# Gated cross-attention and ternary FFN on one core: a schedule moved by one or two slots, and two jobs given to other engines

## What is computed

```
h   = ln(layernorm(x)) ; xq = fp8(clip(h / in_scale))        # four versions: q, qx, k, v
q,qx,k,v = xq @ {wq,wqx,wk,wv}.T ; kx,vx = ctx @ w_kv_x.T     # 16 heads, 8 kv groups, D=128
core = softmax(ln(q) ln(k)^T / sqrt D) v ; xout = softmax(ln(qx) ln(kx)^T / sqrt D) vx
x1  = x + tanh(g0) * (fp8(clip([core, xout] / smooth)) @ wproj.T) * scale
out = x1 + tanh(g1) * down(silu(a) * b), with a,b = quant(layernorm(x1)) @ ternary(w_gate_up).T
```

## Time and profile before

| | |
|---|---|
| median of 3 runs | 1841.8 us (1840.5 to 1842.0) |
| the profiled execution | 1840.5 us, span 1838.4 us |
| busy over the span | PE 1629.0 us (89%), DVE 1536.1 (84%), ACT 1371.2 (75%), POOL 1099.4 (60%) |
| mean granted TensorE clock | 0.971 |
| first `scores` (slot 0) | 111.24 us |
| feed-forward stage | from about 1490 us to the end |

### The profile page before, as it was taken

One profiled execution on the slowest core, in us unless ns is written; L12 is line 12 of the kernel. 1 busy time (PEld: TensorE's weight loads), 2 busy tenths in 40 slices (PEclk: granted clock), 3 DMA queues, 4 the chain that ended last, 5 costly groups with the idle time before them and its releaser, 6 DMA issues.

```text
span 1838.4 us, 35220 instructions
## 1 busy us (share of the span) xinstructions
PE 1629.0 (89%) x11147; PEld 1007.6 (55%) x11164; DVE 1536.1 (84%) x3391; ACT 1371.2 (75%) x3439; POOL 1099.4 (60%) x1421
## 2 busy tenths in 40 slices
PE   2368889889999999999999888999999978999995
PEld 1345555555666665666666555666666534444442
DVE  7568889999897899988788999999988847777774
ACT  6458999879989988998997788989988832222222
POOL 3577888878886787888676667767777520000000
PEclk9889999999999999999999999999999989999998
DMA  3257789779999999999898988999998976322200
GB/s 102 90 148 166 185 189 211 166 181 228 228 227 200 199 242 191 210 232 245 189 222 177 210 195 201 235 226 223 225 232 168 211 166 214 91 73 77 70 18 17
DMA packets 669596, 325.48 MB, mean 177 GB/s; under 512 B 552288, under 2 KB 595424, under 8 KB 669152
## 3 DMA queue, kind: packets, MB, share of 16 engines
q1 hardware_dynamic: 669408, 323.17, 77.5%
HBM read 140.61 MB, written 48.23 MB: 103 GB/s over the span
## 4 chain that ended last, share of the span: by engine, by line
PE 43%; DVE 23%; ACT 13%; POOL 8%; issue 8%; DMA 4%; SPq 0%; ACTq 0%; POOLq 0%; DVEq 0%
PE psum L699 8%; PE psum L654 7%; PE psum L687 7%; PE psum L741 6%; PE psum L716 6%; DVE pp L981 5%; DVE nmx L971 4%; PE psum L661 3%; PE psum L758 3%; DMA pt<-pp 2%; ACT pp L1321 2%; ACT psum L1310 2%; PE psum L674 2%; ACT raw L1241 2%; DVE xh L954 1%
## 5 line engine op out<-in xcount | busy, mean ns | idle before, releaser
L687 PE MATMUL psum<-qk 128*128 128x512 f16 x1536 | 423.6, 385 | 19.5 <-DVE pp L981 13.4
L699 PE MATMUL psum<-pt,vv 128*128 128x512 f16 x1536 | 402.1, 385 | 36.9 <-ACT cy L1329 25.3
L654 PE MATMUL psum<-wbt,xqt 128*128 128x256 f16 (+1 forms) x4096 | 409.2, 249 | 21.5 <-DVE xqt L898 11.1
L1310 ACT ACTIVATE psum<-psum,nmx 128x512 f32<-128x512 f32 x512 | 352.3, 688 | 70.2 <-DVE nmx L971 68.7
L654 PEld LDWEIGHTS psum<-wbt,xqt 128*128 128x128 f16 x4096 | 330.2, 99 | 135.5 <-issue 18.1
L981 DVE SCALAR_TENSOR_TENSOR pp<-psum,prs,pp 128x512 f16<-128x512 f32 x512 | 379.4, 741 | 3.4 <-ACT pp L1321 3.3
L971 DVE TENSOR_REDUCE nmx<-psum 128x1 f32<-128x512 f32 x512 | 345.6, 675 | 31.1 <-PE psum L687 30.6
L1321 ACT ACTIVATE pp<-psum,prs 128x512 f16<-128x512 f32 x512 | 365.7, 714 | 6.7 <-DMA pt<-pp 6.5
L699 PEld LDWEIGHTS psum<-pt,vv 128*128 128x128 f16 x1536 | 147.9, 99 | 236.5 <-issue 55.1
L1564 POOL TENSOR_TENSOR qk<-y,qk 128x512 f16<-128x512 f32 x192 | 232.5, 1211 | 16.0
L687 PEld LDWEIGHTS psum<-qk 128*128 128x128 f16 x1536 | 144.0, 99 | 103.9 <-DVE pp L981 23.1
(11 more groups left out here) (176 smaller groups left out, 2792.8 us busy)
## 6 DMA issues: line engine op xcount, KB each, us to landing
wbt<-ws SPq DMA_DIRECT2D x192, 256.0 KB, 3.7
ws<-wbt SPq DMA_DIRECT2D x64, 256.0 KB, 4.0
catd<-cy SPq DMA_DIRECT2D x64, 256.0 KB, 3.3
raw<-in_wgu SPq DMA_DIRECT2D x64, 256.0 KB, 3.5
raw<-in_w SPq DMA_DIRECT2D x32, 384.0 KB, 3.9
wbt<-catd SPq DMA_DIRECT2D x6, 2048.0 KB, 9.8
pt<-pp SPq DMA_TRANSPOSE x512, 3.8
raw<-in_wp SPq DMA_DIRECT2D x32, 256.0 KB, 3.7
```

Of the source, the lines that this page charges most:

```text
L654: ins = e.matmul(bank[:, o0:o0 + c1 - c0], xv[:, v, kt * 512 + tt * 128:kt * 512 + (tt + 1) * 128], wb[i][:, h, kt, c0:c1], start=kt == 0 ...
L687: ins = e.matmul(SB(n), qk[i][:, jq, u, ss], qk[i][:, jk, w, :], start=k == 0, stop=k == 2)
L699: ins = e.matmul(OB, v[:, t, u, att, :], src[:, w, t, :], start=t == 0 and k == 0, stop=t == 3 and k == 2)
L1310: e.activation(SB(n), SB(n), ACT.Exp, bias=nmx[:, k], accum_out=psm[:, k]).then_inc(s["exp"], 1)
```

## The change

Most edits are numbers in the tables. `FIRST` and the ramp's loads go two slots earlier with `GEMM_AT` (9 to 7), so that the projections of a group come two slots earlier against its scores; one of them, the load of weight tile 3 of group 1, now comes before the two kv loads instead of between them. The first head of a group goes one slot earlier, the x transposes one or two slots later, the second product with v of a head block moves from the second to the third of its four slots. `norm_b` is done by DVE up to B tile 35 (group 8) instead of 7 (group 1), so for 28 tiles the two ACT copies go. In a split job `hi` goes from ACT to POOL and `lo` from POOL to DVE, in the same slots as before.

```diff
-FIRST, PAST = -26, NSLOT + 20
+FIRST, PAST = -28, NSLOT + 20
-PVS = ((0,), (1, 2), (3,), ())
-GEMM_AT = 9
+PVS = ((0,), (1,), (2, 3), ())
+GEMM_AT = 7
-HEADS_AT = (10, 12, 14, 16, 18, 22)
-FACTORS_AT = 6
+HEADS_AT = (9, 12, 14, 16, 18, 22)
+FACTORS_AT = 4
-RAMP_LOAD = (-27, -26, -25, -20, -20, -19)
-W0_AT = -22
+RAMP_LOAD = (-29, -28, -27, -22, -20, -19)
+W0_AT = -24
-STORE_W = 10
+STORE_W = 8
-ACT_NORM = 2 * 4
-WG_AT, CAT_AT, X2_AT = (444, 490), (474, 498), 507
+ACT_NORM = 9 * 4
+WG_AT, CAT_AT, X2_AT = (444, 488), (472, 496), 506
-SCALE_AT = {"sum": 303, "whole": 308, "fac": 309}
+SCALE_AT = {"sum": 303, "whole": 307, "fac": 308}
-    "turn": (19, 24, 35, 51),
+    "turn": (20, 26, 36, 52),
-    "parts": (104, 104, 104, 104),
+    "parts": (102, 102, 102, 102),
@@ sp_program
-                nw, j = divmod(n + 7 + 2 * SLOTS, SLOTS)
+                nw, j = divmod(n + 8 + 2 * SLOTS, SLOTS)
@@ pe_program, gemm
-                            q.wait_ge("w_dn", it * 6 + (6 if it > 1 else 4))
+                            q.wait_ge("w_dn", it * 6 + (6 if it else 4))
@@ dve_program, job: the tern branch as before, and
+                else:
+                    q.wait_ge("l_hi", JV["l_hi", m])
+                    if stored is not None:
+                        q.wait_ge(f"l_st{i}", JV[f"l_st{i}", stored])
+                        q.wait_ge("l_ab", JV["l_ab", summed])
+                    e.tensor_tensor(o.bitcast(F16)[:, 0:512], f, wps[:, j, :], ALU.subtract).then_inc(s["l_lo"], 1)
@@ act_program: job_hi is gone, and its call in slot n
-                e.activation(wps[:, j, :], raw[i][:, 0:512], ACT.Copy).then_inc(s["l_hi"], 1)
@@ pool_program, job: the subtraction is gone; called in slot n instead of n + 1
+                    q.wait_ge(f"raw_ld{i}", JV[f"raw_ld{i}", K0 + m])
+                    e.tensor_scalar(wps[:, j, :], raw[i][:, 0:512], 1.0, 1.0, ALU.mult, ALU.mult).then_inc(s["l_hi"], 1)
```

More of the change, by code:

```diff
@@ L998, in job @@
             def job(m):
-                if JOBS[m][0] != "tern":
+                what, src, j, _ = JOBS[m]
+                i = (K0 + m) % 2
+                f, o = raw[i][:, 0:512], raw[i][:, 512:768]
+                if what in ("sum", "scale"):
                     return
-                i = (K0 + m) % 2
-                f, ob = raw[i][:, 0:512], raw[i][:, 512:768].bitcast(BF16)[:, 0:512]
                 stored, summed = JB[m]
[L1004 to L1008, removed]
+                if what == "tern":
+                    ob = o.bitcast(BF16)[:, 0:512]
+                    q.wait_ge("l_t1", JV["l_t1", m])
+                    q.wait_ge(f"l_st{i}", JV[f"l_st{i}", stored])
+                    q.wait_ge("l_ab", JV["l_ab", summed])
+                    q.done(e.tensor_scalar(ob, f, MAGIC, 1.0, ALU.subtract, ALU.min))
+                    e.tensor_scalar(ob, ob, -1.0, None, ALU.max).then_inc(s["l_t2"], 1)
+                else:
+                    q.wait_ge("l_hi", JV["l_hi", m])
+                    if stored is not None:
+                        q.wait_ge(f"l_st{i}", JV[f"l_st{i}", stored])
+                        q.wait_ge("l_ab", JV["l_ab", summed])
+                    e.tensor_tensor(o.bitcast(F16)[:, 0:512], f, wps[:, j, :], ALU.subtract).then_inc(s["l_lo"], 1)
             def weight_sums():
@@ L1330, in o_out @@
                              scale=f).then_inc(s["o_y"], 1)
-            def job_hi(m):
-                j, i = JOBS[m][2], (K0 + m) % 2
-                q.wait_ge(f"raw_ld{i}", JV[f"raw_ld{i}", K0 + m])
-                e.activation(wps[:, j, :], raw[i][:, 0:512], ACT.Copy).then_inc(s["l_hi"], 1)
             def job(m):
@@ L1416, in act_program @@
                     ctx_hi(b, kt)
-                if JOB_AT.get(n, -1) >= 0 and JOBS[JOB_AT[n]][0] == "split":
-                    job_hi(JOB_AT[n])
                 for at in (n, n - 2):
@@ L1580, in job @@
                 i = (K0 + m) % 2
-                f, o = raw[i][:, 0:512], raw[i][:, 512:768]
                 if what == "split":
[L1583 to L1588, removed]
+                    q.wait_ge(f"raw_ld{i}", JV[f"raw_ld{i}", K0 + m])
+                    e.tensor_scalar(wps[:, j, :], raw[i][:, 0:512], 1.0, 1.0, ALU.mult, ALU.mult).then_inc(s["l_hi"], 1)
             q.wait_ge("pre_v", 1)
@@ L1642, in pool_program @@
                         ctx_lo(b, kt)
-                if JOB_AT.get(n - 1, -1) >= 0:
-                    job(JOB_AT[n - 1])
+                if JOB_AT.get(n, -1) >= 0:
+                    job(JOB_AT[n])
             weights_over(q)
```

## The result

The changed kernel takes 1861.6 us (median, 1856.6 to 1868.2) against 1841.2 for the kernel before on the same chip: ratio 1.0116, 95% interval 1.0098 to 1.0136, so about 21 us slower. I had predicted 1835, with a range of 1823 to 1846.

What follows compares the result with a forecast made beforehand. ScalarE was taken as fullest in groups 1 to 3, 9 and 17, VectorE in 4, 5 and 12 to 14. Terms summed to -7.1 us, giving 1834.7 from the median, predicted as 1835; 8-in-10 range 1823 to 1846.

Steps and rivals of the forecast that it cites:

- ramp and end: Before slot 0 and in groups 30 and 31: gemm parts done earlier, 1.0 us gained at each.
- VectorE has 3 us or more of room in most, so nothing is counted: Groups 7, 8, 10, 11, 15, 16, 18: split subtractions cost nothing; 0.5 us gained in 10 and 11.
- Rival 2: Groups 6, 12 to 14 and 4 to 6: subtractions queue behind GpSimd on full VectorE, 1847 us; chance 0.18.
- the gains in groups 9 and 17: Two and three split copies leave a full ScalarE: gains of 1.5 and 1.7 us, low end 0.
- the 1.05 assumed: Length in us taken for each new VectorE subtraction of a split job, with ends 0.69 and 1.66.
- The rule of the Trainium skill quoted in the prediction: VectorE instructions with two SBUF inputs and GpSimd instructions reading SBUF exclude each other; the second is blocked throughout. No term.
- What the prediction read from ctx_lo: Slow cases of the similar subtraction overlap GpSimd instructions; its spread, 686 to 1662 ns, agrees with mutual blocking.
- the fullest engine plus a smaller loss: Groups 1 to 3: time is the fullest engine plus 2 or 1 us per group; gains 4.3 and 4.7 us.
- rival 1: Groups 1 to 3: wait moves to the broadcast, VectorE bounds at once; gain 3 instead of 9, 1841 us; chance 0.20.
- their work is the same and stands at the same distance from it: Tables `FACTORS_AT`, `STORE_W`, `load_w`, `parts`, `SCALE_AT` follow the gemm, so they were counted at nothing.
- PVS at nothing: Last `pv` of a block ends 0.65 us later; counted as nothing, 6 to 12 us kept for the range.
- slot 0 at 110.0 (near 110): End of the ramp: slot 0 near 110 was listed as a sign that the forecast was right.
- rival 3: Groups 0 to 3, 9, 17 and ramp: stops vanish, TensorE's clock rises, bigger gain, 1824 us; chance 0.16.

Runs made afterwards that it cites:

- the run with the copy put first: Kernel before with only the split jobs moved, GpSimd's rounding copy first in its slot instead of last: 1844.8 us, +0.38% against the kernel before.
- 103: Changed slot tables alone, with the four ctx_hi copies of a block in slot 103 instead of 102: 1844.8 us, +0.31% against the kernel before.
- 104: Changed slot tables alone, with the ctx_hi copies back in slot 104 instead of 102: 1847.0 us, +0.39% against the kernel before.
- turn in 25: Changed slot tables alone, with the second x transpose of a batch in slot 25 instead of 26: 1847.3 us, +0.46% against the kernel before.
- the two runs with a head moved: Changed slot tables alone, with a group's last head in slot 23 instead of 22 (1854.8 us), or its second in 13 instead of 12 (1859.5 us).

## Why the prediction was wrong

Sorted by part, the sum on record was -7.1 us for `norm_b` (-4.3 - 4.7 + 2.2 + 0.7 of group 6 - 1.0), +2.0 for the split jobs (+5.0 + 0.7 - 1.5 - 0.5 - 1.7) and -2.0 for ramp and end. Measured alone: +2.4, +12.1 and +8.8. All three failed, each by about 10 us. (The interval of the first reaches from 0 to 4.8, so it may have cost nothing; the gain didn't come.)

- **The split jobs: "VectorE has 3 us or more of room in most, so nothing is counted".** This step priced VectorE's work by its room over a group. With the split jobs alone the seven groups counted so (7, 8, 10, 11, 15, 16, 18) took 5.6 us more, where the sum had -0.5; groups 12 to 14 took 7.3 more for 5.0, group 6 2.1 for 0.7. Room is a sum over 16 slots, and the subtraction stands ahead of the reciprocal on which ScalarE's next slot hangs. In the changed kernel the mean was 1.08 us (34.6 us in 32), as assumed; the waits for GpSimd added 9.3, and in groups 6 to 18 ScalarE's wait for the reciprocal grew from 7.4 to 39.0 us (27.1 with the split jobs alone, 10.8 with the copy left on ScalarE). Before, then after:

```profile
ACT prs L1316 <- DVE psm L976: 7.4, 14, 1.4
```

```profile
ACT prs L1325 <- DVE psm L976: 39.0, 35, 3.2
```

  That VectorE now stands behind GpSimd's last instruction of a slot could be read from the order of the instructions, and I didn't follow it. Rival 2 had the direction, and its sign (groups 12 to 14 at 138 or more: 139.6) came; its condition (a mean above 1.5) did not. Of the gains in groups 9 and 17, that of 17 came with the split jobs alone (1.9 us for 1.7), that of 9 didn't (0.6 longer). That the mean came out at the 1.05 assumed is in part luck: the same instruction has 0.99, 0.83 and 0.82 in the three other kernels that have it on VectorE.
- **Who blocks whom.** The rule of the Trainium skill quoted in the prediction (page "SBUF — State Buffer", section "Who interferes with whom") agrees with the trace of the changed kernel. GpSimd has an instruction running beside every one of the 32 subtractions, the short ones too, so it is the order that decides. VectorE first, then GpSimd first:

```profile
609.26 0.68 DVE L1017 TENSOR_TENSOR raw<-raw,wps 128x512 f16<-128x512 f32 x1
609.33 1.62 POOL L1566 TENSOR_TENSOR qk<-y,qk 128x512 f16<-128x512 f32 x1
...
539.88 1.20 POOL L1566 TENSOR_TENSOR qk<-y,qk 128x512 f16<-128x512 f32 x1
540.00 1.63 DVE L1017 TENSOR_TENSOR raw<-raw,wps 128x512 f16<-128x512 f32 x1
```

  In all 11 subtractions of 1.63 or 1.64 us GpSimd's L1566 or L1578 had begun 0.07 to 0.38 us before; five of the 15 short ones run beside L1566, which began after them or at most 0.02 before, and then L1566 took 1.57 to 1.71 us instead of its median of 1.16. So a short subtraction isn't free: GpSimd pays for it, and no term of the sum had that. (Two cases in the run with the copy put first don't fit by their starts: L1566 began 0.33 and 0.39 before, took 2.03 and 2.09, and the subtraction 0.67.) The page's other half, that an instruction with at most one SBUF input doesn't contend, holds by the page only outside the 2-port modes; here the new `norm_b`, which reads PSUM, took 405 to 425 ns throughout, although one of GpSimd's subtractions or additions of 128 x 512 or more ran beside it in 23 of 36 cases. What the prediction read from ctx_lo was no sign yet: all six of its cases overlap GpSimd instructions, the short ones too.
- **norm_b: the fullest engine plus a smaller loss.** I wrote that removing one stop gives a longer wait at the next, and then took 2.35 us per group of it as gained because the other stop was to be moved as well. Alone, it went exactly as warned (3.8 to 5.4), and groups 1 to 3 gained 1.9 us of the 9.0 counted, while groups 4 to 6, where VectorE is full, lost 9.4 in that long execution (2.9 counted). Groups 2 and 3 of the changed kernel take 91.7, near the 90.7 forecast, but they take 92.6 with the new slots alone: most of that gain was the slots'. ScalarE is still the fullest there (85.2 to 84.6), VectorE 92% and not 97% full. Group 1, forecast 46.3, took 54.0, all of it from the new slots (54.0 with them alone): slot 12 waits 3.5 us for ScalarE's reads of the second x transpose. So groups 1 to 3 are unchanged in sum, which was the sign of rival 1, but by a loss in one and a gain in two, and not by its mechanism.
- **The tables at nothing: "their work is the same and stands at the same distance from it".** This failed most plainly: for the gemm, the heads, the x transposes and what follows the gemm the sum had only the 2 us of ramp and end, and they cost 17 us. The distance to the gemm was kept, the one to ScalarE's own fixed work was not: `ctx_hi` (2.2 us) moved from behind the `o_out` copy of slot 103 to ahead of it. Slots repeat by 4 for `o_out`, by 16 for heads and tiles; a shift by 2 changes who stands beside whom. With the new slots alone the losses stand in group 1 (3.4 us), in group 6 (3.4), in 12 to 14 (6.7) and in the full groups (5.0), against gains in 2, 3, 9, 17 and 19 to 22. Five runs each moved one piece to remove a stop; the stop went, others grew, and the time came down by 3 us at most (103), stayed (104, turn in 25) or rose (the two runs with a head moved). So it is shown that these tables together cost 17 us, and that their stops change places. That ScalarE's order is what does it is argued from the stops, not shown; the gemm, the heads and the x transposes were never moved one by one from the kernel before, so which of them is the root stays open.
- **PVS at nothing.** It gains 5 us alone and 8 in the new slots. The cause is only argued: the four slots of a block, where TensorE doesn't wait, took 2.4, 2.2, 3.3, 2.2 us and with `PVS` alone take 2.4, 2.2, 2.6, 2.8 (in the new slots the third takes 3.0 instead of 3.7), so the longest is shorter, which suits engines with as much work in each slot. I had asked only whether its last product comes later.
- **Right:** slot 0 at 110.0 (near 110); ramp and end about 1 us each; groups 23 to 29 unchanged (277.5 to 277.0); the subtraction's mean length, with the luck said above; VectorE as the loser of groups 4 to 6. Rival 1's stop at the broadcast didn't come, that wait halved; rival 3's clock of 1.00 in groups 2 and 3 neither (0.98).

## What to carry to other kernels

Work given to an engine with room is priced by what stands behind it in that engine's line and by whom it must wait for, not by the engine's share of a group: an instruction that stands ahead of a hand-off, here of the reciprocal for which ScalarE's next slot waits, can pass on its wait and its length however much room the engine has over the group. Before moving a table of slots, list for every moved piece what it passes on its own engine, modulo each period of the schedule; keeping its distance to its producer is only half of it. Measure the parts of a bundled change apart: here `PVS`, which was held to be nothing, gained, the other tables lost, and the two moves between engines, for which the longest arguments were made, gained nothing.

## What the runs showed of the hardware

The same subtraction on VectorE (two SBUF inputs, 128 x 512) took 0.68 to 0.69 us in 15 of the 32 cases of the changed kernel, 1.03 to 1.09 in six and 1.63 or 1.64 in 11. GpSimd was at work beside all of them. In the 11 long cases its instruction with two SBUF inputs of that size had begun first, in the six middle ones its rounding copy L1560, by 0.06 to 0.13 us. Where the subtraction began first, GpSimd's L1566 took 1.57 to 1.63 us instead of 1.16.

A subtraction that has waited for a GpSimd instruction starts 0.06 to 0.07 us after GpSimd's next one (all 11 cases). Six of these 11 took 1.63 us, one 1.09 and four 0.69, where the next one was small; of the 21 that had not waited five took 1.63 or 1.64. The median was 1032 ns in the changed kernel and 682 with the copy put first in the old slots.
